# A fused mixture-of-experts, state-space and mixture-of-experts kernel: one TensorE signal per slot of the feed-forward, loads placed earlier among the stores, no powers between the scatter blocks

## The reference, cut to what matters

```
x = x + 0.5 * ffn(layernorm(x))
x = x + attn(layernorm(x))          # projection, short convolution, state-space scan, gate, norm, projection
x = x + 0.5 * ffn(layernorm(x))

def ffn(x):                         # the same weights both times
    scores = sigmoid(x @ router.T)  # 16 experts, 4 groups of 4
    ...                             # the best 2 groups, in them the best 4 experts
    w = 2.5 * scores[best] / sum(scores[best])
    routed = sum over the 4 of w[e] * (silu(x @ gate[e].T) * (x @ up[e].T)) @ down[e].T   # width 128
    shared = (silu(x @ sh_gate.T) * (x @ sh_up.T)) @ sh_down.T                            # width 256
    return routed + shared
```

## Time and profile before

| | |
|---|---|
| runs, us | 1678.22, 1679.23, 1689.73 (median 1679.23) |
| profiled execution: its own time, its span | 1694.23, 1692.4 |
| mean granted TensorE clock | 0.899 of full speed |
| busy: PE, DVE, ACT, POOL | 80%, 53%, 39%, 56% of the span |
| routed pairs of stage 1: first gate matmul, last | 178.4, 545.8 |
| routed pairs of stage 2: first gate matmul, last | 1232.5, 1624.8 |
| GpSimd's indirect DMAs: 256 scatters, 256 gathers | 253.8 and 263.0 busy |
| GpSimd's powers between scatter blocks | 46, 27.2 busy |

### The profile page before, as it was taken

The page is one execution under the profiler, slowest core; times in us unless marked ns, Lnnn a source line. Parts: engine busy times, 40 slices in busy tenths (PEclk is TensorE's granted clock), DMA queues, the critical chain, the costliest instruction groups (busy, mean ns, idle before and its releaser), DMA issues.

```text
span 1692.4 us, 22687 instructions
## 1 busy us (share of the span) xinstructions
PE 1345.6 (80%) x6904; PEld 1143.0 (68%) x6904; DVE 905.1 (53%) x2190; ACT 658.4 (39%) x1088; POOL 951.7 (56%) x1002
## 2 busy tenths in 40 slices
PE   5847577968959969999999999969564599696890
PEld 5736465857847747888888887857554488585780
DVE  5626251224436798888888878765353122352453
ACT  2222232423424445656656665523311134242330
POOL 2664835054264668878878977417466701634535
PEclk9869788989989979999999999989687899798895
DMA  9951344546555520001000000234324435565633
GB/s 362 401 185 66 112 144 143 168 154 200 191 182 182 185 89 13 26 15 38 26 26 25 25 23 11 87 131 168 113 103 140 149 118 171 164 212 187 196 131 99
DMA packets 86917, 218.39 MB, mean 129 GB/s; under 512 B 16272, under 2 KB 28560, under 8 KB 85904
## 3 DMA queue, kind: packets, MB, share of 16 engines
q1 hardware_dynamic: 62224, 149.82, 25.1%
q0 software_dynamic: 24576, 67.14, 12.5%
HBM read 109.43 MB, written 107.48 MB: 128 GB/s over the span
## 4 chain that ended last, share of the span: by engine, by line
PE 54%; DVE 16%; issue 15%; another core or an unknown queue 9%; ACT 3%; POOL 2%; DVEq 0%; POOLq 0%; DMA 0%; ACTq 0%
PE ps L1025 14%; PE ps L1054 9%; PE ps L993 5%; PE ps L1030 5%; DVE at_xs L1784 3%; PE ps L1984 3%; PE ps L1986 3%; PE ps L1985 3%; PE ps L2045 2%; PE ps L1038 2%; DVE f_xin L791 2%; PE ps L1009 2%; PE ps L2046 1%; PE ps L2034 1%
## 5 line engine op out<-in xcount | busy, mean ns | idle before, releaser
L452 POOL DMA_INDIRECT f_gbuf<-yg,f_rows x256 | 263.0, 1027 | 389.8 <-DMA yg<-f_yo 243.7
L426 POOL DMA_INDIRECT xg<-f_xn,f_rows x256 | 253.8, 991 | 180.1 <-DVE f_rows L719 110.0
L1025 PE MATMUL ps<-f_wgu,f_xT 128*128 x1248 | 322.9, 405 | 17.9 <-issue 15.2
L1054 PE MATMUL ps<-f_wd,f_hT 128*128 x624 | 181.2, 417 | 144.2 <-issue 81.9
L1025 PEld LDWEIGHTS ps<-f_wgu,f_xT 128*128 128x128 f32 x1248 | 244.9, 207 | 53.1 <-issue 22.1
L768 DVE TENSOR_TENSOR f_h<-ps,f_sg 128x256 f32<-128x256 f32 x156 | 66.1, 424 | 377.8 <-ACT f_sg L503 242.1
L1054 PEld LDWEIGHTS ps<-f_wd,f_hT 128*128 128x128 f32 x624 | 124.3, 205 | 175.9 <-issue 159.1
L490 ACT COPY f_xT<-ps 128x512 f32<-128x512 f32 x212 | 124.2, 586 | 219.6 <-remote 100.0
L503 ACT ACTIVATE f_sg<-ps 128x256 f32<-128x256 f32 x156 | 60.1, 385 | 289.6 <-PE ps L1025 160.9
L1030 PE MATMUL ps<-f_xT,f_wgu_sh 128*128 128x256 f32 x512 | 135.2, 422 | 24.7 <-issue 12.0
L1784 DVE SCALAR_TENSOR_TENSOR at_xs<-at_raw,at_taps,at_xs 128x512 f32<-128x512 f32 x136 | 138.4, 1020 | 6.9 <-POOL at_xs L1435 4.2
(11 more groups left out here) (258 smaller groups left out, 2655.7 us busy)
## 6 DMA issues: line engine op xcount, KB each, us to landing
f_xq<-xg SPq DMA_DIRECT2D x78, 512.0 KB
yg<-f_yo SPq DMA_DIRECT2D x156, 256.0 KB
xg<-f_gbuf SPq DMA_DIRECT2D x39, 512.0 KB, 5.9
f_wgu<-in_gate_up SPq DMA_DIRECT2D x4, 1280.0 KB
f_xin<-in_x SPq DMA_DIRECT2D x8, 512.0 KB, 7.0
xg<-f_xn,f_rows POOLq DMA_INDIRECT x256
f_gbuf<-yg,f_rows POOLq DMA_INDIRECT x256
x<-f_xin SPq DMA_DIRECT2D x8, 512.0 KB, 4.1
```

What stands on the lines that cost most here:

```text
L426: G.indirect_dma_start(xg[0:USED[g] * P, :], bass.IndirectOffsetOnAxis(ap=rows[g][:, b, k:k + 1], axis=0), xn[:, SUB * TILE0[g] + b, :], N ...
L452: G.indirect_dma_start(gbuf[:, n % GBUF, k, :], None, yg[0:USED[g] * P, :], bass.IndirectOffsetOnAxis(ap=rows[g][:, b, k:k + 1], axis=0), ...
L1025: last = T.matmul(gu_ps[:, j % 2, s * 2 * P:(s + 1) * 2 * P], x_of(k, s, d), weight(wgu[:, :, d, :], experts[s]), start=(d == 0), stop=(d ...
L1054: last = T.matmul(y_ps[:, yy % 2, s * D:(s + 1) * D], hT[:, i % 4, s * P:(s + 1) * P], weight(wd if kind == "routed" else wd_sh, experts[i ...
```

## The change

1. After the six `route` events at the start, the events are cut into **slots**, one for each unit (a pair, or half of a shared event) or for a `route` event. In a slot TensorE does: the `down` that is due, the `turn_h` that is due, the `turn_x` that is due, the router, and last `gate_up`. Only the slot's last instruction gives a signal, `slot_done`. ACT and DVE wait for the slot and then do what belongs to it. `gu_ready`, `h_ready`, `hT_in_psum`, `hT_done` and `y_in_psum` are gone; `gated` and `hT_copied` (DVE) are new.
2. The distances grow: `turn_x` two slots ahead of its event's first (`AHEAD`), `turn_h` two slots after its unit (it was one), `down` of a pair four slots after (it was two units), of a shared event three.
3. SP issues 7 loads before the first store (it was 4), and then one after every second store as before, so each is three places earlier in its order.
4. The combinations of the first two gathered groups stand at slots, 8 slots after the last pair that they need and then 8 in 5 slots for 5 blocks; `store_tile` follows by the same table.
5. `REST_SCATTER` is (0, 0, 0): no powers between scatter blocks. The third group's list of experts is packed after pair 11 instead of 9.

```diff
-REST_SCATTER = (2, 1, 1)
+REST_SCATTER = (0, 0, 0)
+START = HEAD - 1
+AHEAD = 2
+TURN_H = 2
+DOWN_ROUTED = 4
+DOWN_SHARED = 3
+COMBINE = 4
-def combine_at(g, b):
-    return USED[g] // 2 + 4 + 8 * b // 5
+class Slots:
+    def __init__(self, events):
...
+        for k in range(START, len(events)):
+            kind, n = events[k]
+            self.first[k] = len(self.slots)
+            for u in range(max(1, UNITS_OF[kind])):
+                slot = Slot(k, u == 0, u + 1 >= UNITS_OF[kind])
...
+        for k in range(START + 1, len(events)):
+            self.slots[self.turned_in(k)].turns.append(k)
...
+            if routed:
+                self.slots[self.of_unit[slot.unit] + TURN_H].turn_h = slot.unit
+            at = self.of_unit[slot.unit] + (DOWN_ROUTED if routed else DOWN_SHARED)
...
+            self.slots[at].down = yy
+    def turned_in(self, k):
+        return max(self.first[k] - AHEAD, 0)
+    def combine(self, g, b):
+        return self.of_pair(USED[g] // 2 - 1) + DOWN_ROUTED + COMBINE + 8 * b // 5
+    def stored_ahead_of(self, g, b):
+        late = [n for n in range(sum(RP)) if self.of_pair(n) + DOWN_ROUTED >= self.combine(g, b) + 1]
+        return late[0] if late else sum(RP)
@@ load_quad, the order of SP
-                sp.wait_ge(xT_in_psum, at_event["routed", routed_pair(2 * (load - XQ) + 1)] + 1)
+                sp.wait_ge(slot_done, SLOTS.turned_in(at_event["routed", routed_pair(2 * (load - XQ) + 1)]) + 1)
-        for q in range(XQ):
+        pairs = sum(RP)
+        early = (DOWN_ROUTED + AHEAD) // 2
+        for q in range(XQ + early):
             load_quad(q)
...
         for n in range(pairs):
             store_y(n)
-            if n % 2 == 0 and XQ + n // 2 < pairs // 2:
-                load_quad(XQ + n // 2)
+            if n % 2 == 0 and XQ + early + n // 2 < pairs // 2:
+                load_quad(XQ + early + n // 2)
@@ scalar
+        for s, slot in enumerate(SLOTS.slots):
...
+            act.wait_ge(slot_done, s + 1)
+            if slot.unit is not None:
+                silu(slot.unit)
+            for k in slot.turns:
+                take_xT(k)
+            if slot.down is not None and OUTPUTS[slot.down][0] == "routed":
+                take_y(slot.down)
@@ vector
+            if slot.unit is not None:
+                gate(slot.unit)
+            if slot.turn_h is not None:
+                take_hT(s, slot.turn_h)
+            if slot.down is not None and OUTPUTS[slot.down][0] != "routed":
+                take_part(s, slot.down)
+            for g in range(NG - 1):
+                for b in range(GB[g]):
+                    if SLOTS.combine(g, b) == s:
+                        combine(g, b)
@@ tensor
         def gate_up(j, k, experts):
             pe.wait_ge(xT_ready, k + 1)
-            if j >= 2 and UNITS[j - 2][0] != "routed":
-                pe.wait_ge(hT_done[j % 2], j // 2)
+            if j >= 2:
+                pe.wait_ge(gated, j - 1)
...
-            last.then_inc(gu_ready, 1)
+            return last
...
+            if slot.down is not None:
+                last = down(slot.down, experts)
+            if slot.turn_h is not None:
+                last = turn_h(slot.turn_h)
+            for ahead in slot.turns:
+                last = turn_x(ahead)
+            if kind in ("route", "both") and slot.first:
+                last = router(k, n)
...
+                last = gate_up(j, k, ex)
...
+            last.then_inc(slot_done, 1)
```

More of the change, by code:

```diff
@@ L1 @@
 from contextlib import ExitStack
+from dataclasses import dataclass, field
 import math
@@ L293, in outputs_before, with after_event @@
         return sum(kind in kinds for kind, _ in OUTPUTS[0:yy])
[L295 to L316, removed]
+    SLOTS = Slots(EVENTS)
+    UNITS = SLOTS.units
+    def after_event(k):
+        return START if k < START else k + 1
     def sync(sp, other):
@@ L528, in scalar @@
             yield
-        j = 0
-        for k, (kind, n) in enumerate(EVENTS):
-            if fresh and (kind, n) == ("route", 5):
+        for k, (kind, n) in enumerate(EVENTS[0:START]):
+            if fresh and n == 5:
                 squash(0)
-            if (kind, n) in (("shared", 4), ("routed", (0, 0))):
-                next(other, None)
-            if k + 1 < len(EVENTS):
-                take_xT(k + 1)
-            if not fresh and k + 1 < HEAD:
+            take_xT(k + 1)
+            if not fresh:
@@ L932, in vector, with after @@
             yield
[L934 to L947 removed]
+        def after(k):
+            kind, n = EVENTS[k]
             for g in range(NG):
                 if (kind, n) == COUNT_AT[g]:
[L950 removed]
+                    copy_counts(g, after_event(k))
                 if (kind, n) == PACK_AT[g]:
[L952 removed]
+                    copy_words(g, after_event(k))
             if fresh:
@@ L967, in vector @@
                 next(other, None)
-        take_part(OUTPUTS[-1][1], len(OUTPUTS) - 1)
+        for k in range(START):
+            if fresh and EVENTS[k] == ("route", 5):
+                for i in range(3):
+                    route_piece(0, i)
+            after(k)
+        for s, slot in enumerate(SLOTS.slots):
+            if slot.first and EVENTS[slot.event] == ("routed", (0, 0)):
+                next(other, None)
+            if slot.unit is not None:
[8 more added lines that the diff above has]
+                        combine(g, b)
+            if slot.last:
+                after(slot.event)
         for b in range(len(FINAL), GB[2]):
@@ L1095, in tensor @@
                     pe.wait_ge(w_in[piece], 32)
-            for u in range(UNITS_OF[kind]):
+            if slot.down is not None:
[6 more added lines that the diff above has]
+                last = router(k, n)
+            if j is not None:
                 if j == 0:
```

204 lines of the change are left out of this document (109 added, 95 removed).

## The result

The changed kernel takes 1752.72 us (median, 1741.04 to 1756.79) where the kernel before, on the same chip, takes 1684.48 us (1678.22 to 1694.87): ratio 1.0444, 95% interval 1.0388 to 1.05. The forecast was 1514. The profiled execution took 1752.57 us, its span is 1750.6, 58 us over the span before.

A forecast was written before the change was run, and what follows sets the result against it. TensorE was taken as bound by its signals passing slowly while GpSimd issues DMAs. Gains of 148 us beside pairs and 27 in heads, less 10 in tails, make 165: 1694.2 becomes 1529, median 15 lower, 1514 us; range 1445 to 1650.

The forecast's parts named there:

- Part 1: Pairs beside GpSimd's DMAs: TensorE's signals queue at 3.7 us each; one per slot cuts losses, 249 to 101 us, gaining 148.
- Part 5: Scatters without powers: each power costs GpSimd 0.48 us, 46 cost 22, mostly off the path; 3.7 us a signal assumed throughout.
- Rival (c): First group's scatters: powers let signals through; without them 84 us lost against 43, tails +10, total 1730 us; chance 0.08.
- Heads: Beside the first group's scatters: fewer signals gain 19 us of TensorE idle time and a better clock 8, together 27.
- Part 2: Stage ends: longer distances delay the last down and so the last gather, costing 5 us a stage, 10 in all.
- Part 3: SP's order: second group's first load holds up stores, so TensorE waits near pair 10; costs 10 us stage 2, 3 stage 1.
- Part 4: Combinations of gathered groups at their new slots: cost nought, from -5 to +10 us; a late gather makes DVE hold slots.
- Attention: Attention stage, where GpSimd issues no indirect DMAs: forecast to keep its time.
- The signs: Trace signs of being right: pairs 3.3 to 5 us in runs, clock over 0.95, pair stretches about 300 and 315 us.
- (a): Beside GpSimd's DMAs: delay belongs to each signal, 8 us lag, not a queue; gain 31 us, 1648 us; chance 0.14.
- (b): GpSimd's runs: signals wait for the run to pause, whatever their number; nothing moves, 1684 us; chance 0.10.
- The rule of the skill: Against the signal saving: an increment on a matmul's completion costs about 26 ns, so 546 saved signals give 14 us at most.

The follow-up runs named there:

- E2: Kernel before with only its 46 scatter powers taken out, where the kernel before takes 1700.34 us: 1764.26 us, ratio 1.0393.
- E1: Changed kernel with the scatter powers (2, 1, 1) put back, where the kernel before takes 1688.46 us: 1694.52 us, ratio 1.0044.
- slots with powers: Changed kernel with the scatter powers (2, 1, 1) put back; ratio to the kernel before 1.022 to 1.0241 at about 1441 us, 1.0044 at 1688.46.
- short distances with powers: Changed kernel with old load order, turn of h after 1 slot, downs after 2, and scatter powers put back: 1440.28 us, 0.9997 of the kernel before.
- short distances without powers: Changed kernel with old load order, turn of h after 1 slot, downs after 2: 1436.02 us (0.9956 of the kernel before) and 1776.34 us (1.052).

## Why the prediction was wrong

**Two steps failed.** The forecast was 239 us too low. 171 of them are Part 1 and what is built on it: a gain of 165 us was forecast, and with the powers kept the change lost 6 (1.0044). The other 67 turn that nothing into a loss (1.0444 without the powers, 1.0044 with them; 64 us by the kernel before alone), and they are one sentence in Part 5: "Whether the signals of an unbroken scatter come slower than one in 2.7 us, the trace shows only for gathers (3.2); I have used 3.7 for all." The powers' pauses were priced as 0.48 us of GpSimd time to be gained, not as what bounds TensorE's wait. Measured: 42.19 and 48.63 us for one pair in an unbroken scatter.

Rival (c) named the mechanism of Part 5's miss, with 1730 us and a chance of 0.08, and its number is near the 1753 partly by luck. It put the whole loss beside the first group's scatters, 42 us for each of the two. Beside that of stage 1 TensorE is idle 30.9 us of 67, where it was idle 25.5 of 71. The loss lies beside the second group's scatters: 42.36 us idle instead of 10.97 ahead of the pairs of stage 1, and 28 us more in the pairs of stage 2 (392.3 to 420.6 in E2), which (c) had unchanged. It took a scatter's pace from the gathers'; but a gather run there pauses by itself, for a free buffer, after 20 DMAs and 26 us (24 and 31 at most), and a group of 48 scatters without powers has no pause for 61 us.

**Part 1, the queue with a slow server: wrong, and it held the forecast.** The earlier trace rows were read as one signal in 2.7 to 4.3 us by dividing the time by the signals that passed. The division gives such a number whatever the mechanism is; what would have told them apart was a run with another number of signals, and the trace of before has none. With a quarter of the signals two pairs of the same run take 23.96 us instead of 25.65. The predicted gain of 148 us beside the pairs is at most 15 (367.4 + 392.3 against 355.0 + 389.6 in E1), or some 33 by an estimate that adds back the 18 us which distances and loads cost the pairs in the prompt comparison below. The reading that TensorE's signals are late was right (one is 44.7 us late in the changed kernel); that their number sets how late was not. Part 1 also counted the second group's scatter as beside the pairs in both stages, and in stage 1 it began at 145.2, 33 us before the first pair.

**Heads: wrong in sign.** Forecast a gain of 27. The first head lost 49 (178.4 to 227.2), nearly all of it by the powers: 180.7 with them, 227.6 with them taken from the kernel before. Only some 6 us of it had gathered when the second group's scatter began (150.9 against 145.2); the rest came beside that scatter. The 30 us that the pairs of stage 1 win after belong to the same account: the scatter is over by then.

**Part 2 and Part 3 right.** The two prompt traces, slots with powers against short distances with powers, give the terms: between the stages 694.4 against 687.4 and at the end 66.8 against 63.2, so 7.0 and 3.6 where the forecast had 5 each (the first stretch has other work in it too). In the changed kernel the last gather starts 17.4 us after the last gate matmul instead of 13.4, 4 us, forecast 5. The pairs cost 5.2 us in stage 1 and 12.5 in stage 2, forecast 3 and 10. The 13th pair of stage 2 takes 30.98 us instead of 3.25, and 11 of that are given back three pairs later: the step to the first pair that needs the second scatter, with two shared events in it, is 16.01 instead of 27.33. (The two kernels differ in the place of gate-and-up in the slot too.) Together 30.6 us of span with the first gate's 2.4, forecast 23. In starved comparisons that pause lies beside the starvation, and holding the load was worth 6 us, not resolved.

**Part 4: small.** DVE's combinations wait 31.1 us in both stages together (L844, above), most of it for gathers, where that line had 12.4 before; the forecast was 0, from -5 to +10 a stage. What of it is on the path wasn't tested. **Part 5's 0.48 us** for a power is right (0.47 by 70 of them) and, in the prompt comparison, so is "off the path": 0.999. **Attention** kept its time: the stretch between the stages has 14 us more in E1 and 7 in the prompt pair of traces, both with the later last gather in them, and was not taken apart further.

**The signs.** Of those named, the clock of the pair stretches is 0.89 and 0.85, not over 0.95; the stretches take 337.1 and 408.6 us, not 300 and 315; the two slots in each long gather run still take 8.2 to 15.5; the heads are longer, the sign of (c).

**The rivals.** (a), a constant lag for each signal, 8 us in its sum: no, ACT's waits for a slot in one kernel run up to 50.4 us. (b), nothing moves because a run costs the same whatever the number of signals: right for the slots (1.0044 with powers), and "whatever their number" was the better reading of the earlier trace rows. What was missing is that (b) and (c) go together: if the number of signals doesn't count and the length of an unbroken run does, taking out the pauses costs time. That signals wait for the pause itself is too strong: in the changed kernel one arrives at 1332.38, with three DMAs of the run still to come. (b) and (c) together had 0.18.

**The rule of the skill.** The extra signals cost nothing that is resolved: 1441.03 against 1440.28 us for about the 546 that Part 1 counted, given back, and 1434.69 against 1436.02. The Trainium skill, "TensorE: Matmul & The Clock Gate", section "The cost: per-tile semaphore tail", has about 26 ns for each (its own case is matmuls on tiles of the array), an estimated 14 us at most; the runs, all of them prompt, are under that bound, and the rule's verdict that signals are cheap was the better guide to this change. Whether it holds in a starved comparison was not run; 42.19 us with four and 48.63 with one speak for it.

**What stays open.** What makes a comparison starved or prompt: the record numbers the chips, and one number gave 1440 us twice and then 1688; whether it is the same piece each time isn't known, so time is a rival to the chip. Another rival is untested, the recording of the profile itself. All times on record are of executions with a recorded clock, and the starved traces are the ones that lack records: of slots with powers the starved trace holds 10794 updates of semaphores and the prompt one 18500, and the page gives the loads from `xg` a time to landing only in the prompt one:

```profile
f_xq<-xg SPq DMA_DIRECT2D x78, 512.0 KB
```

```profile
f_xq<-xg SPq DMA_DIRECT2D x78, 512.0 KB, 4.5
```

Nor is it shown why TensorE's signals and the starts of its instructions are late beside these DMAs, nor how a pause lets them through; no starved run has pauses of another number or length. The best version depends on the kind of comparison: short distances without powers gain 0.4% prompt and lose 5.2% starved. The one that loses nowhere it was run is short distances with powers, 0.9997 prompt, not run starved; the kernel before is the safe choice.

## What to carry to other kernels

An instruction that computes nothing may be a pause that another engine lives on: before it is removed, look for who makes progress right after it, and price the longest unbroken run that is left, not the instruction. A rate got by dividing a stretch by its events is no mechanism; ask which run with another number of events would give another stretch. And a loss that depends on a second engine's stream should be measured in more than one comparison, at other hours and on other chips, before a kernel is tuned to it.

## What the runs showed of the hardware that was not expected

- One file, 1441 us in one comparison and 1684 to 1700 us in another, 17% apart, nearly all of it in the stages with GpSimd's indirect DMAs: slots with powers reach the first gate at 144.8 us prompt and 180.7 starved, and have 266.5 and 300.1 us of pair stretches prompt, 355.0 and 389.6 starved, while the stretch between the stages differs by 6 us (694.4, 700.7) and GpSimd's own DMAs take the same time:

```profile
L470 POOL DMA_INDIRECT xg<-f_xn,f_rows x256 | 254.0, 992 | 177.6 <-DVE f_rows L771 107.6
```

```profile
L470 POOL DMA_INDIRECT xg<-f_xn,f_rows x256 | 254.4, 994 | 128.7 <-issue 70.6
```

The first is starved, the second prompt: 992 and 994 ns for one.

- A signal of TensorE that came 44.7 us late beside an unbroken row of indirect DMAs, and TensorE idle for 43.71 us behind it. With pauses of about 0.5 us after every fourth or eighth DMA ACT's longest wait is 12.77 us; 46 such pauses are worth 3.9% (1.0393) there and nothing (0.999) in a prompt comparison.
- Starts of single matmuls that wait for nothing, 1.4 us apart beside the same DMAs (95.26, 96.65, 98.05).
- In the stretch of that late signal (1275 to 1337) the granted clock was lower with more idle time of TensorE: 0.61 with 16.05 us busy of 62, against 0.76 with 36.22 of 68.
